# Layer-norm variances of the output stage and feed-forward: four one-column products and a round trip through DRAM replaced by one broadcast product of 512 columns

## The reference

```python
def _layernorm(x, axis=-1, eps=1e-05):
    m = jnp.mean(x, axis=axis, keepdims=True)
    v = jnp.var(x, axis=axis, keepdims=True)
    return (x - m) / jnp.sqrt(v + eps)

h = _L0_tok_ref(x, ...)
h = h + _L0_attn_ref(_layernorm(h, axis=-1), ...)     # its last step is vals @ w_o.T + b_o
h = h + _L0_ffn_ref(_layernorm(h, axis=-1), ...)

# _L0_ffn_ref: 16 heads, 64 -> 256 -> 64 channels each
t = x.reshape(b * l, Dm)[:, perm].reshape(b * l, h, d)
t = jnp.einsum('bhd,hdm->bhm', t, up)
t = jax.nn.gelu(t, approximate=False)
t = jnp.einsum('bhm,hmd->bhd', t, down)
```

## Time and profile before

| | |
|---|---|
| median of 3 executions | 983.7 us (983.49 to 984.62) |
| profiled execution | 982.39 us |
| its span | 980.7 us |
| busy: TensorE, VectorE, ScalarE, GpSimd | 956.6, 510.6, 425.8, 401.5 us |
| granted TensorE clock, mean over the span | 0.993 |
| output stage, about | 744 to 847 us |
| feed-forward, about | 847 to 970 us |

### The profile page before, as it was taken

The page is one execution under the profiler, slowest core; times in us unless marked ns, Lnnn a source line. Parts: engine busy times, 40 slices in busy tenths (PEclk is TensorE's granted clock), DMA queues, the critical chain, the costliest instruction groups (busy, mean ns, idle before and its releaser), DMA issues.

```text
span 980.7 us, 15765 instructions
## 1 busy us (share of the span) xinstructions
PE 956.6 (98%) x6132; PEld 714.6 (73%) x6132; DVE 510.6 (52%) x841; ACT 425.8 (43%) x756; POOL 401.5 (41%) x324
## 2 busy tenths in 40 slices
PE   9999999999999999999999999999999999999996
PEld 7878787777777888788778878878887877533331
DVE  6253535868458312356475166156063567859451
ACT  6245454373544543446253243243132232467553
POOL 1225252444542112823560550551023288668632
PEclk9999999999999999999999999999999999999998
DMA  8651909096354264149003002100223966724521
GB/s 287 240 174 2 218 3 234 5 167 191 98 196 126 67 132 173 43 156 338 1 12 99 21 11 67 53 12 22 57 75 129 307 260 230 263 88 130 182 76 65
DMA packets 74920, 122.89 MB, mean 125 GB/s; under 512 B 29143, under 2 KB 38359, under 8 KB 70878
## 3 DMA queue, kind: packets, MB, share of 16 engines
q1 hardware_dynamic: 68686, 104.93, 36.3%
q0 software_dynamic: 5120, 16.78, 5.0%
q10 hardware_dynamic: 1040, 0.16, 0.1%
HBM read 79.36 MB, written 42.50 MB: 124 GB/s over the span
## 4 chain that ended last, share of the span: by engine, by line
PE 83%; POOL 5%; DVE 4%; issue 3%; DMA 2%; ACT 2%; POOLq 0%; SPq 0%; ACTq 0%; DVEq 0%
PE bank L333 21%; PE bank L335 20%; PE bank L334 20%; PE bank L1880 6%; PE bank L1889 6%; PE bank L1632 2%; POOL vacc L369 2%; POOL wf_l L327 2%; PE bank L1603 1%; POOL acc L397 1%; DVE sq L414 1%; PE bank L1762 1%; DMA hg<-h_s,rows 1%; PE bank L1789 1%; DVE h L1432 1%
## 5 line engine op out<-in xcount | busy, mean ns | idle before, releaser
L369 POOL TENSOR_TENSOR vacc<-vacc,sq 128x512 f32<-128x512 f32 x72 | 97.3, 1352 | 44.0 <-ACT sq L419 30.8
L333 PE MATMUL bank<-cv_h,wf_h 128*128 128x512 f32 x256 | 104.5, 408 | 0.0
L333 PE MATMUL bank<-xa_h,wp_h 128*128 128x512 f32 x256 | 102.6, 401 | 0.7 <-DVE xa_l L1154 0.7
L335 PE MATMUL bank<-xa_h,wp_l 128*128 128x512 f32 x256 | 100.3, 392 | 0.0
L334 PE MATMUL bank<-xa_l,wp_h 128*128 128x512 f32 x256 | 100.3, 392 | 0.0
L335 PE MATMUL bank<-cv_h,wf_l 128*128 128x512 f32 x256 | 100.0, 391 | 0.0
L334 PE MATMUL bank<-cv_l,wf_h 128*128 128x512 f32 x256 | 99.9, 390 | 0.0
L1135 ACT ACTIVATE gt<-bank 128x512 f32<-128x512 f32 x128 | 66.1, 603 | 53.0 <-PE bank L1880 53.0
L741 POOL TENSOR_TENSOR fo<-fo,res 128x512 f32<-128x512 f32 x32 | 42.8, 1351 | 106.0 <-ACT fo L887 76.6
L1880 PE MATMUL bank<-dd,up_f 64*128 64x512 f32 x256 | 63.6, 615 | 0.9 <-DVE h L1432 0.9
L1889 PE MATMUL bank<-gt,dn_f 128*64 128x512 f32 x256 | 61.8, 604 | 0.0
(11 more groups left out here) (180 smaller groups left out, 2184.2 us busy)
## 6 DMA issues: line engine op xcount, KB each, us to landing
xs<-x_t SPq DMA_DIRECT2D x32, 256.0 KB, 6.1
h_s<-ho SPq DMA_DIRECT2D x8, 1024.0 KB, 8.0
res<-h_s SPq DMA_DIRECT2D x32, 256.0 KB, 3.6
h_s<-fo SPq DMA_DIRECT2D x32, 256.0 KB, 2.4
dc<-h_s SPq DMA_DIRECT2D x4, 2048.0 KB, 8.7
h<-h_s SPq DMA_DIRECT2D x8, 1024.0 KB, 7.6
h_s<-h SPq DMA_DIRECT2D x8, 1024.0 KB, 4.8
band_s<-zero SPq DMA_DIRECT2D x4, 1072.0 KB, 8.3
```

Source lines behind the costliest of these rows:

```text
L333: pe.matmul(o, wh, xh, start=start, stop=False)
L335: return pe.matmul(o, wl, xh, start=False, stop=stop)
L369: g.tensor_tensor(vacc[:, :], t[:, 0, :] if k == 1 else vacc[:, :], t[:, at, :], ALU.add).then_inc(ln_vac, 1)
```

## The change

Variances of the four chunks that enter the feed-forward are no longer made as four columns. `row_var_pe` multiplies `vacc` with the whole of `mean_w`, 512 columns wide, so every partition gets the variance of every token, as for the mean. `row_std_act` takes the root of the whole bank straight into `rtd`. `row_recip_dve` takes the reciprocal of 128 of its columns, four calls for one chunk. The store of the reciprocal root, its load, and the two waits of `d_stat_load` for it are gone; SP's queue keeps the mean's store and load. `rtd[1]` lies at another address, since it is written while the output stage's weights are still in use at the old one. The reciprocals stand in VectorE's program: chunk 0's between the four first centres of the last output chunk, with the four scales moved behind the first group's evacuation; chunk 1's in feed-forward steps 0 to 3, ahead of everything but `d_add`; chunk 2's in steps 8 to 11, ahead of the centres of chunk 3; chunk 3's in steps 16 to 19. A scale waits for all four. The first stage of the kernel keeps the four-column form.

```diff
-        rtd = [place(f"rtd{i}", [P, N], F32, at) for i, at in enumerate((E + 50 * KIB, R2 + 10 * KIB))]
+        rtd = [place(f"rtd{i}", [P, N], F32, at) for i, at in enumerate((E + 50 * KIB, LNT + 8 * KIB))]
...
+        def row_var_pe(pe, L, b):
+            since(pe, ln_vac, L, 7, 7)
+            pe.matmul(bank[b][:, :], mean_w[:, :], vacc[:, :], start=True, stop=True).then_inc(ln_var, 1)
...
+        def row_std_act(act, L, b):
+            n = L - 2 * CH
+            since(act, ln_var, L, 1, 1)
+            if n >= 2:
+                act.wait_ge(xd_sc, 8 * (n - 1))
+            act.activation(rtd[n % 2][:, :], bank[b][:, :], ACT.Sqrt, bias=eps[:, 0:1]).then_inc(ln_std, 1)
...
+        def row_recip_dve(v, L, i):
+            r = rtd[L % 2][:, i * P:(i + 1) * P]
+            since(v, ln_std, L, 1, 1)
+            v.reciprocal(r, r).then_inc(ln_rstd, 1)
...
@@ SP: stat_store
-                    sp.wait_ge(ln_rstd, S + 1 if S < CH - 1 else S + CH + 2)
...
-                        sp.dma_start(stat_s[S, 1].rearrange("(p t) -> p t", t=TILES), rstd4[:, :]).then_inc(rstd_st, 16)
...
@@ SP: d_stat_load
-                sp.wait_ge(rstd_st, 16 * (CH + n))
...
-                sp.dma_start(rtd[n % 2][:, :], stat_s[CH - 1 + n, 1].partition_broadcast(P)).then_inc(d_ld[n % 2], 16)
...
-                if 0 < c < CH - 1:
-                    stat_store(CH + c - 2, 1)
...
-            stat_store(2 * CH - 3, 1)
...
-            stat_store(2 * CH - 2, 1)
...
@@ ScalarE, output stage and feed-forward
-                    stat_std_act(act, L, VAR_BANK)
+                    row_std_act(act, L, VAR_BANK)
...
-                    stat_std_act(act, L - 1, FF_VAR_BANK)
+                    row_std_act(act, L - 1, FF_VAR_BANK)
...
@@ VectorE, d_prep and d_scale
+            def d_center(n, k):
+                v.wait_ge(g_ld[n % 2][k], 16 * (n // 2 + 1))
+                v.wait_ge(d_ld[n % 2], 16 * (n // 2 + 1))
...
             def d_scale(n, k):
+                v.wait_ge(ln_rstd, 2 * CH + TILES * (n + 1))
...
@@ VectorE, output stage
                 if c == CH - 1:
-                    d_prep(0, range(4))
+                    for k in range(4):
+                        d_center(0, k)
+                        row_recip_dve(v, 2 * CH, k)
                 o_evac(c, A_GROUPS[0])
...
                 if c == CH - 1:
+                    for k in range(4):
+                        d_scale(0, k)
                     d_prep(0, range(4, KB))
                 o_evac(c, A_GROUPS[1])
...
-                if 0 < c < CH - 1:
-                    stat_recip_dve(v, 2 * CH + c - 1)
...
@@ VectorE, feed-forward
+                if s < TILES:
+                    row_recip_dve(v, 2 * CH + 1, s)
                 if 0 <= n < CH - 1:
                     d_prep(n + 1, [k])
                 for i, steps in enumerate(CENTERS):
                     o_center(CH - 2 + i, steps.get(s, ()))
-                    if s == VAR_AT[i] + 2:
-                        stat_recip_dve(v, 3 * CH - 2 + i)
+                    if 0 <= s - VAR_AT[i] - 2 < TILES:
+                        row_recip_dve(v, 3 * CH - 2 + i, s - VAR_AT[i] - 2)
...
@@ TensorE, output stage and feed-forward
-                            stat_var_pe(pe, 2 * CH + c - 1, CH + c - 2, VAR_BANK)
+                            row_var_pe(pe, 2 * CH + c - 1, VAR_BANK)
...
-                        stat_var_pe(pe, 3 * CH - 2 + i, 2 * CH - 3 + i, FF_VAR_BANK)
+                        row_var_pe(pe, 3 * CH - 2 + i, FF_VAR_BANK)
```

More of the change, by code:

```diff
@@ L430, in stat_var_pe, with stat_std_act @@
             for t in range(TILES):
[L431 to L435, removed]
+                mm = pe.matmul(bank[b][:, t:t + 1], vacc[:, t * P:(t + 1) * P], mean_w[:, 0:1],
                                start=True, stop=True)
             mm.then_inc(ln_var, 1)
-        def stat_std_act(act, L, b=LN_BANK):
+        def row_var_pe(pe, L, b):
+            since(pe, ln_vac, L, 7, 7)
+            pe.matmul(bank[b][:, :], mean_w[:, :], vacc[:, :], start=True, stop=True).then_inc(ln_var, 1)
+        def stat_std_act(act, L):
+            b = LN_BANK
             since(act, ln_var, L, 1, 1)
-            since(act, rstd_st, (L - CH - 1 if L >= 2 * CH else L) - 1, 16, 16)
-            if L < CH:
-                since(act, sm5, L - 1, 8, 1)
+            since(act, rstd_st, L - 1, 16, 16)
+            since(act, sm5, L - 1, 8, 1)
             act.activation(rstd4[:, :], bank[b][:, 0:TILES], ACT.Sqrt, bias=eps[:, 0:1]).then_inc(ln_std, 1)
+        def row_std_act(act, L, b):
[4 more added lines that the diff above has]
+            act.activation(rtd[n % 2][:, :], bank[b][:, :], ACT.Sqrt, bias=eps[:, 0:1]).then_inc(ln_std, 1)
         def stat_recip_dve(v, L):
@@ L482, in stat_store @@
                 else:
-                    sp.wait_ge(ln_rstd, S + 1 if S < CH - 1 else S + CH + 2)
[L484 to L487, removed]
-                        sp.dma_start(stat_s[S, 1].rearrange("(p t) -> p t", t=TILES), rstd4[:, :]).then_inc(rstd_st, 16)
+                    sp.wait_ge(ln_rstd, S + 1)
+                    sp.dma_start(stat_s[S, 1].rearrange("(t p) -> p t", p=P), rstd4[:, :],
+                                 allow_slow_non_contiguous=True).then_inc(rstd_st, 16)
             def a_store(c, g):
@@ L1143, in _ @@
                 if s == VAR_AT[0] + 1:
-                    stat_std_act(act, L - 1, FF_VAR_BANK)
+                    row_std_act(act, L - 1, FF_VAR_BANK)
                     stat_copy_act(act, L, 2 * CH - 2)
                 if s == VAR_AT[1] + 1:
-                    stat_std_act(act, L, FF_VAR_BANK)
+                    row_std_act(act, L, FF_VAR_BANK)
         @block.vector
@@ L1445, in o_center @@
                     stat_center(v, 2 * CH + c, CH + c - 1, k, h2[c % 2][:, k, :])
+            def d_center(n, k):
+                v.wait_ge(g_ld[n % 2][k], 16 * (n // 2 + 1))
+                v.wait_ge(d_ld[n % 2], 16 * (n // 2 + 1))
+                if n > 0:
+                    v.wait_ge(up_mm, 32 * (n - 1) + 4 * k + 4)
+                v.tensor_tensor(dd[:, k, :], hg[n % 3][:, k, :], mtd[n % 2][:, :],
+                                ALU.subtract).then_inc(d_cent, 1)
             def d_prep(n, ks):
                 for k in ks:
[L1451 to L1456, removed]
+                    d_center(n, k)
                 for k in ks:
```

## The result

The changed kernel takes 988.53 us (median of 7 executions, 987.22 to 992.24) against 983.97 us for the kernel before in the same session: a ratio of 1.0052, 95% interval 1.0033 to 1.0071. It is slower by 4.6 us, where no clear change had been forecast. The profiled execution took 987.22 us with a span of 985.0 us, 4.3 us more than the span of before.

The account below looks back on a forecast made before the run. The chain was taken to run over GpSimd and VectorE in the output stage, TensorE alone in the feed-forward. Terms: -2.0 + 0 + 1.1 + 1.3 = +0.4 us on 983.7, giving 984.1 us; 8-in-10 range 981.5 to 986.6.

Parts of the forecast that it names:

- (b): VectorE, feed-forward steps 0 to 3: 0.86 us more per step fits within the 3.78 us step, so 0.
- (c): VectorE, feed-forward steps 8 to 11: reciprocals ahead of the centres make squares and gelus late, +1.3 us.
- rival 3: TensorE's clock falls in a gap ahead of the feed-forward, +1.7 us, 985.8; half-speed stretch near 820 may go; chance 0.12.
- (a): VectorE, last output chunk: four reciprocals between centres delay the last evacuations, +1.1 us, from -1.5 to +2.2.
- The product in the feed-forward: TensorE, two feed-forward sites: one variance product of 0.96 us replaces four pieces taking 1.96, -2.0 us.
- The output stage's products: TensorE, output stage: 1.0 us less twice, but hidden behind waits for GpSimd and VectorE, worth nothing.
- SP's queue: Output stage: without the reciprocal store the values load issues some 8 us sooner, worth 0 (-0.5 to +0.5).
- ScalarE's root: ScalarE: root over 512 columns takes 0.690 instead of 0.264 us, +0.43 four times, covered in the feed-forward.
- Rival 2: Feed-forward steps 10 to 13: late squares become the bound, +2.8 us, 986.5; chance 0.14.
- The signs: Prediction wrong if mean product at 800.33 moves over 0.5, reciprocals are not near 0.95, or clock falls after 843.

Follow-up runs that it names:

- experiment 10: The kernel before with only SP's load of chunk 3's values put ahead of the reciprocal store and its wait: ratio 1.0006 to the kernel before.
- experiment 8: The changed kernel with ten extra 512-column matmuls on TensorE in its gap ahead of the feed-forward: ratio 1.0043 to the kernel before.
- experiment 1: The changed kernel with the reciprocals of feed-forward steps 0 to 3 and 8 to 11 behind the centres: ratio 1.0003 to the kernel before.
- experiment 2: The changed kernel with the eight reciprocals of feed-forward steps 0 to 3 and 8 to 11 only 4 columns wide, same places: ratio 1.0009 to the kernel before.
- experiment 4: The kernel before with eight spare 128-column reciprocals added ahead of the centres in feed-forward steps 0 to 3 and 8 to 11: ratio 1.0055 to the kernel before.
- experiment 7: Kernel of experiment 1 with a 4-column reciprocal after each of twelve two-input VectorE instructions in the last output chunk: ratio 0.9982 to the kernel before.

## Why the prediction was wrong

It was wrong in direction and size: 984.1 us with a range to 986.6, measured 988.5, a change of +4.6 us where +0.4 was forecast. The step that failed is (b), "Feed-forward steps 0 to 3": put at 0, it cost 2.0 us, because each centre waited out a GpSimd add. Next to it, (c) was mis-sized by 1.8 us for the same reason, and rival 3's fall of the clock, left out of the sum, cost 0.8; (a) came out 0.35 under. With 0.1 missing on the products and 0.2 in two transitions, that is the way from the forecast's +0.4 to the profile's +4.9.

- **The product in the feed-forward** was right: -2.0 forecast, -1.9 in the changed chain; alone in the kernel before -2.6 us with an interval of -0.7 to -4.3.
- **The output stage's products, SP's queue, ScalarE's root:** forecast at 0. The chain there goes over the same sums with the same lengths, and the load sent early alone gave nothing (experiment 10). ScalarE's root ends before the next thing it waits for (first site: at 878.53, with the mean product over at 878.66). Right, as far as the runs can tell.
- **(a) the last output chunk:** +1.1 forecast, 0.75 in the profile. Right in mechanism. With some luck: the centres were to take 2.4 and the last scales 5.08, and they took 4.07 and 3.58, since GpSimd's sum began one instruction sooner and met the last centre and one scale instead of two scales. Moving the reciprocals away took off 1.6 to 2.3 us by the ratios, with the clock's share in it, and the intervals overlap.
- **(b) steps 0 to 3:** forecast 0, measured 2.0 us. I added up lengths: 2.4 us of free instructions and 0.86 more in a step of 3.78. But in the earlier trace rows and in the changed profile a two-input instruction is not free while GpSimd adds. Before, the centres of these steps ran in the time in which GpSimd issues the scatter that the step's first VectorE instruction releases. The adds come behind that scatter, so they hang on the same instruction, a fixed time behind it; 0.86 us of delay moves the centres out of the one and into the other. In steps 2 and 3 each centre then waits out an add; in step 1, with one add, both come behind it (2.99 us). I had seen this exclusion in (a) and (c), and did not ask for it where the sum of lengths fitted.
- **(c) steps 8 to 11:** +1.3 forecast, 3.1 measured. Right in kind, mis-sized for the same reason: I let one centre in each of steps 10 and 11 meet an add; in the changed profile the pair takes about 2.4 us in each of steps 9, 10 and 11 instead of 1.28. My range for it ended at 2.4.
- **Rival 2** (late squares bind the feed-forward) is what happened, and in a part of the stage where I had not placed it. I priced it at +2.8 with a chance of 0.14.
- **Rival 3** (the clock falls ahead of the feed-forward) happened too, in both profiles of the changed kernel, at 0.8 and 1.1 us instead of 1.7; I forecast a gap of 2.5 us, and TensorE waited 1.9. Only the profiles show its price; the timed comparison (experiment 8) doesn't resolve it. The rival's other half held as well: behind the 512-column product the half-speed stretch at 820 us is gone (the clock is 1.00 from 819.0 to 823.2 in the changed profile), but that this was worth nothing there is argued and not tested.
- **The signs:** of the three that were to show the prediction wrong, the clock's fall came; the mean product moved by 0.57 us, over the 0.5 allowed, but ahead of the change; the reciprocals were as forecast. The variance products took 1.06 us and not 0.96, and the mean product behind the first one 0.86, so the pair's sum was as forecast.

Shown by runs: the eight reciprocals' place ahead of the centres makes the loss (experiments 1, 2 and 4). That it is GpSimd's adds that the centres wait for is read from the traces, where a centre that waits ends 0.55 to 0.57 us behind the end of an add in each of steps 1 to 3 and 9 to 11; no run took the adds away. The Trainium skill, "SBUF — State Buffer", section "Who interferes with whom", states that exclusion for two-input VectorE instructions beside a GpSimd instruction that reads SBUF, and these traces agree; it also says that one input doesn't contend, and the reciprocals, at 0.93 to 0.95 us everywhere, agree as well.

Open: what makes the hold of a gather (experiment 7), and how often it comes. The Trainium skill ("SBUF — State Buffer", same section) holds, as an inference, that descriptor generation and a `tensor_tensor` do not exclude each other. The profiles are divided: in two a gather's issue ends 0.9 us behind a run of twelve of them, and in three gathers inside such a run take 0.95 us.

## What to carry to other kernels

An instruction added to an engine with idle time is not priced by its length. Ask what stands behind it, and what another engine does at the time into which that is pushed; if the two engines exclude each other and the other one's work is released by the same event, a small delay can turn a fixed gap into a meeting in every step. Where a one-input instruction and a two-input one are both due, the two-input one goes first while the other engine is busy with something that doesn't exclude it, and the one-input one beside the adds. Test an unexpected loss by moving the instruction before shortening it: here moving was worth as much as leaving it out.

## What the runs showed of the hardware

- A reciprocal of 128 columns takes 0.93 to 0.95 us, as the straight line between 4 and 512 columns said.
- A centre that starts in the last half microsecond of GpSimd's scatter issue (857.84 against an end at 858.34) does not run ahead of the add that starts at 858.37: its square starts only at 860.24, behind that add. In step 9 the first centre starts at 889.37, 0.60 us ahead of the add at 889.97, and its square starts at 890.03: it was first, and only the second centre waited.
- A gather's issue can last 6.97 us instead of 0.95 with the DMA engines nearly idle (their share was 0.20 from 838 to 842 us in experiment 1).
- In the three profiles that have the four one-column products in the output stage (before, experiments 4 and 10) TensorE's granted clock was 0.60 to 0.65 on average from 820 to 824 us, just behind the second of them. In the nine that have the 512-column product it was 1.00 there.
- Single executions of one kernel spread over more than the differences looked at here (984.97 to 990.61 us in experiment 8); the split between late evacuations and the clock rests on profiles for that reason.
